# Two attention blocks on one core: scores with all maxima in one block, values in one run, and the steps around them moved

## The chip, the core and the metric

The kernel runs on one core of a Trainium2 chip. A core has five engines that run beside each other and wait for each other through semaphores: TensorE (PE in the profile) does matmuls into PSUM, VectorE (DVE) and ScalarE (ACT) work element by element and can read PSUM, GpSimd (POOL) works element by element in SBUF, and SyncE (SP) issues DMAs. Each engine takes its instructions strictly in the order of the program. The metric is the time of one execution on the device in microseconds.

## What is computed

`x` has 4 images of 64 channels by 32 x 32 positions. Two layers follow each other. Each one does this (cut from the reference of layer 0; layer 1 is the same but for the names and eps = 1e-6):

```python
h = group_norm(x, norm_w, norm_b)            # 32 groups, 2 channels each
q = einsum('bhwc,cd->bhwd', h, Wq) + bq      # k and v likewise
scores = einsum('bnc,bmc->bnm', qf, kf) * C ** (-0.5)     # 1024 x 1024 per image
attn = softmax(scores, axis=-1)
o = einsum('bnm,bmc->bnc', attn, vf)
o = einsum('bnc,cd->bnd', o, Wo) + bo
return x + o
```

## The kernel before

**Units.** An image in a layer is a unit; there are 8, numbered 0 to 7 (`LAST` = 7). A unit of the second layer needs the result of the same image in the first, four units earlier. The code runs in windows `w`: in window w the scores of unit w are computed, the maxima of unit w+1 and the preparation of unit w+2.

**A unit on TensorE.** The 1024 x 1024 scores are cut into 8 tiles of 128 keys by 1024 queries. `scores(u, t)` makes one tile by 8 matmuls (L846 to L863), six of them for the products of high and low parts of q and k and two that add the negative maximum of each query (`q_row`) to it. ScalarE then takes the exponential (`exp`, L442) from PSUM into `probs[t]`. `values(u, t)` (L878) multiplies the values with `probs[t]` and sums over the tiles in `ps_attn`. `project` and `project_v` make q, k and v of a unit from the normed image `h`.

**Maxima.** The maximum of each query has to be known before its scores tile is finished. `partial_max(u, m)` (L808, L809) computes one eighth of the scores in a single pass, and VectorE's `part` (L588) reduces it. All go through one PSUM buffer, `ps_max`, so that TensorE's next maximum waits for VectorE's reduction. After eight, `join` takes the maximum over the parts, TensorE turns the result (`turn_max`, L822), ScalarE stages it in `max_rows` (`stage_max`, L430), and SyncE's `place_rows` (L239) puts it into `q_row` by two DMAs.

**Denominators.** The sum of the eight `probs` of a unit is built by one addition on VectorE (`first_add`, L618, tiles 0 and 1) and six on GpSimd (`add`, L315, tiles 2 to 7; the code's number t is the tile's). An exponential of the next unit may write `probs[t]` only when the addition of the old one is done. `denominators` (L893) sums over the keys on TensorE after all six additions, `reciprocal` (L626) inverts on VectorE, and `spread_rden` sends the result to all channels by eight DMAs into `rden`: six issued by SyncE (L249) and two by ScalarE (L458), or all eight by SyncE for units 0 and 6. GpSimd's `finish` (L321, L324), the final step, multiplies by `rden` and adds the image. For units 5 to 7 VectorE does it (`finish_tail`, `finish_last`).

**Norm.** VectorE makes the statistics (`own_stats`, `share_stats`, `join_stats`), GpSimd takes the inverse square root (`root`, L296), VectorE makes gain and shift (`affine`), ScalarE applies them (`apply_norm`) and gives `h`.

**Order.** It is all written out by hand. On TensorE, in a window, scores, maxima and values alternate: two tiles of scores, a maximum, one to three tiles of values, and so on; tiles 6 and 7 of the values of unit w-1 come in window w. On GpSimd the root of unit w+2 comes first, then additions 2 to 5, `finish(w-1)`, additions 6 and 7. On SyncE comes `spread_rden(w-1)`, then the exchange DMAs of unit w+2 (`swap_hi`, `swap_lo`, which fill `cross`), then `place_rows(w+1)`.

Of the kernel before, what the change touches and what calls it, by code (L numbers as in the profile page):

```python
# [11 lines left out]
P = 128  # L12
# [18 lines left out]
def attention_pair(nc, x, layer_params, consts, out):  # L31
# [20 lines left out]
    with ExitStack() as ctx:  # L52
# [53 lines left out]
        ps_attn = psum("ps_attn", [P, HALF])  # L106
        ps_misc = psum("ps_misc", [P, HALF])
# [98 lines left out]

        def scores_buffer(unit, t):
            return ps_scores[t % 2] if unit < LAST else (ps_scores[0], ps_scores[1], ps_max)[t % 3]
# [4 lines left out]
        def _(sp):  # L213
# [53 lines left out]
            for w in range(UNITS):  # L267
                if w:
                    spread_rden(w - 1)
# [3 lines left out]
                if w + 1 < UNITS:  # L273
                    place_rows(w + 1)
# [6 lines left out]
        def _(pool):  # L281
# [53 lines left out]
            root(2)  # L335
            for w in range(UNITS):
                if 3 <= w + 2 < UNITS:
                    root(w + 2)
                for t in range(2, 2 + pool_adds(w)):
                    add(w, t)  # L340
                    if t == 5 and 0 < w < LAST - 1:
                        finish(w - 1)

        @block.scalar
        def _(act):
# [35 lines left out]
            def high_front(u):  # L381
                act.wait_ge(params_in[u // B], 16)
                act.wait_ge(proj_mm, u + 1)
                act.activation(front[u % RING][:, HI], ps_scores[0][:, HI], ACT.Identity,
                               bias=layer[u // B][:, BIAS_QK:BIAS_QK + 1]).then_inc(front_hi, 1)

            def high_back(u):
                act.wait_ge(back_set, u // B + 1)
                act.activation(back[u % RING][:, HI], ps_scores[0][:, LO], ACT.Identity,
# [87 lines left out]
            for w in range(UNITS):  # L477
                prep = w + 2 < UNITS
                exp(w, 0)
                exp(w, 1)  # L480
                if 0 < w < LAST:
                    copy_v(w + 1)
                if 0 < w < LAST:
                    copy_attn(w - 1)
                exp(w, 2)
                if w == LAST:
                    copy_attn(w - 1)
                exp(w, 3)
                if prep:
                    apply_norm(w + 2)  # L490
                exp(w, 4)
                exp(w, 5)
                if prep:
                    high_front(w + 2)
                    high_back(w + 2)
                if 1 < w < LAST:
                    spread_rden(w - 1)
                if 0 < w < LAST:
# [3 lines left out]
                exp(w, 6)  # L502
                exp(w, 7)
                if w == 0:
                    stage_max(1)
# [8 lines left out]
        def _(dve):  # L514
# [55 lines left out]
            def low_front(u):  # L570
                dve.wait_ge(front_hi, u + 1)
                dve.scalar_tensor_tensor(out=front[u % RING][:, LO], in0=ps_scores[0][:, HI],
# [4 lines left out]
            def low_back(u):  # L577
                dve.wait_ge(back_hi, u)
                dve.scalar_tensor_tensor(out=back[u % RING][:, LO], in0=ps_scores[0][:, LO],
# [4 lines left out]
            def part(u, m, ps=ps_max):  # L584
# [36 lines left out]
            def reciprocal(u):  # L621
                sums = ps_misc[:, 0:P] if u < LAST else ps_max[:, HALF:HALF + P]
# [74 lines left out]
            part(1, 0)  # L697
            own_stats(2)
            part(1, 1)
            share_stats(2)  # L700
            part(1, 2)
# [475 lines left out]
```

## Time and profile before

| | us |
|---|---|
| median of 3 runs | 186.3 (185.76 to 186.8) |
| the profiled execution | 186.09 |
| its span, from the first to the last instruction | 184.3 |
| TensorE busy | 177.0 (96%) |
| VectorE busy | 132.4 (72%) |
| GpSimd busy | 121.4 (66%) |
| ScalarE busy | 100.3 (54%) |

The span is what the trace shows; some 1.8 us of the execution lie outside it. The busy share of an engine alone does not say whether it bounds the kernel. The chain of waits does: it starts at the last instruction and goes back, at each step to whatever released it or to the instruction before it on its engine. The granted clock of TensorE was 0.997 of full speed on average.

### The profile page before, as it was taken

To read this page: it belongs to the slowest core of one execution; us is meant where nothing else is said; L and a number is where in the kernel's file an instruction comes from. 1 tells how busy PE (TensorE), PEld (TensorE's weight loads), DVE (VectorE), ACT (ScalarE), POOL (GpSimd) and SP (SyncE) were. 2 spreads that over 40 slices of the span, in tenths; PEclk is the share of its full clock that TensorE was granted. 3 is DMA by queue.
4 is the path that set the end of the run, shared out by engine and by line. 5 is a ranking of instruction groups with operands and counts; after the bars stand their busy time and mean duration, and the time that the engine had idled before them with its cause. 6 is when DMAs were issued, how large, how long until landed. Compare 5 with 4: busy or idle time off the path is not lost.

```text
span 184.3 us, 3436 instructions
## 1 busy us (share of the span) xinstructions
PE 177.0 (96%) x1295; PEld 96.2 (52%) x1295; DVE 132.4 (72%) x200; ACT 100.3 (54%) x137; POOL 121.4 (66%) x79
## 2 busy tenths in 40 slices
PE   7988899999999999999999999999999999999993
PEld 3445545545535655455535655555535555456671
DVE  2789987679867686859676785769675586484743
ACT  4289367616656376446666476426656554466500
POOL 3265016996799929997699949996799939705000
PEclk9999999999999999999999999999999999999998
DMA  5534100500025000420024001600025101010111
GB/s 152 190 78 107 43 5 0 114 4 2 0 50 124 3 0 18 114 44 0 4 70 102 0 0 31 146 4 0 1 66 111 57 0 46 16 57 16 44 57 57
DMA packets 8896, 8.90 MB, mean 48 GB/s; under 512 B 1656, under 2 KB 5936, under 8 KB 8880
## 3 DMA queue, kind: packets, MB, share of 16 engines
q1 hardware_dynamic: 7648, 7.90, 17.5%
q10 hardware_dynamic: 1232, 0.79, 1.5%
q8 instruction: 10, 0.16, 0.4%
q14 instruction: 6, 0.05, 0.1%
HBM read 1.58 MB, written 1.05 MB: 14 GB/s over the span
## 4 chain that ended last, share of the span: by engine, by line
PE 90%; DVE 8%; issue 1%; POOL 0%; ACT 0%; DVEq 0%; POOLq 0%
PE ps_attn L878 28%; PE ps_max L808 10%; PE ps_scores L846 8%; PE ps_scores L862 7%; PE ps_scores L850 7%; DVE part_max L588 7%; PE ps_scores L848 7%; PE ps_scores L787 4%; PE ps_scores L774 3%; PE ps_misc L795 3%; PE ps_misc L893 2%; PE ps_attn L885 2%; PE ps_misc L885 1%; PE ps_misc L822 1%; PE ps_scores L849 1%; PE ps_scores L863 1%
## 5 line engine op out<-in xcount | busy, mean ns | idle before, releaser
L315 POOL TENSOR_TENSOR prob_sum<-prob_sum,probs 128x1024 f32<-128x1024 f32 x41 | 97.6, 2379 | 29.0 <-ACT probs L442 16.8
L588 DVE TENSOR_REDUCE part_max<-ps_max 128x2 f32<-128x1024 f32 x60 | 73.4, 1223 | 31.3 <-PE ps_max L809 30.9
L442 ACT ACTIVATE probs<-ps_scores 128x1024 f32<-128x1024 f32 x62 | 61.0, 1026 | 46.1 <-PE ps_scores L863 45.4
L878 PE MATMUL ps_attn<-probs,vals 128*64 128x512 f32 x224 | 54.5, 605 | 0.0
L878 PEld LDWEIGHTS ps_attn<-probs,vals 128*64 128x64 f32 x224 | 13.5, 136 | 26.5 <-issue 17.9
L862 PE MATMUL ps_scores<-q_row,ones_r 64*128 64x512 f32 x62 | 24.5, 396 | 0.5 <-ACT q_row L424 0.5
L863 PE MATMUL ps_scores<-q_row,ones_r 64*128 64x512 f32 x62 | 24.6, 396 | 0.0
L808 PE MATMUL ps_max<-back,front 64*128 64x512 f32 x31 | 14.0, 450 | 1.4 <-DVE part_max L588 1.4
L808 PE MATMUL ps_max<-cross,front 64*128 64x512 f32 x29 | 14.7, 505 | 0.3 <-DVE part_max L588 0.3
L809 PE MATMUL ps_max<-cross,back 64*128 64x512 f32 x29 | 14.6, 505 | 0.0
L809 PE MATMUL ps_max<-front,back 64*128 64x512 f32 x31 | 14.0, 451 | 0.0
L296 POOL TENSOR_TENSOR rstd<-var_eps,minus_half 128x1 f32<-128x1 f32 x8 | 4.4, 554 | 13.4 <-DVE var_eps L543 13.4
L862 PEld LDWEIGHTS ps_scores<-q_row,ones_r 64*128 64x128 f32 x62 | 11.4, 184 | 3.2 <-issue 0.7
L847 PE MATMUL ps_scores<-back,cross 64*128 64x512 f32 x31 | 13.0, 418 | 0.0
L846 PE MATMUL ps_scores<-front,back 64*128 64x512 f32 x31 | 12.9, 416 | 0.0
L847 PE MATMUL ps_scores<-back,front 64*128 64x512 f32 x31 | 12.4, 400 | 0.0
L846 PE MATMUL ps_scores<-front,cross 64*128 64x512 f32 x31 | 12.4, 399 | 0.0
L851 PE MATMUL ps_scores<-back,cross 64*128 64x512 f32 x31 | 12.2, 392 | 0.0
L850 PE MATMUL ps_scores<-front,back 64*128 64x512 f32 x31 | 12.1, 391 | 0.0
L851 PE MATMUL ps_scores<-back,front 64*128 64x512 f32 x31 | 12.1, 390 | 0.0
L849 PE MATMUL ps_scores<-back,cross 64*128 64x512 f32 x31 | 12.1, 390 | 0.0
L850 PE MATMUL ps_scores<-front,cross 64*128 64x512 f32 x31 | 12.1, 390 | 0.0
(157 smaller groups left out, 365.8 us busy)
## 6 DMA issues: line engine op xcount, KB each, us to landing
cross<-front SPq DMA_DIRECT2D x16, 128.0 KB, 2.3
cross<-back SPq DMA_DIRECT2D x16, 128.0 KB, 2.3
rden<-block_rden SPq DMA_DIRECT2D x46, 32.0 KB, 1.9
xs<-x_dram SPq DMA_DIRECT2D x4, 256.0 KB, 4.6
out_dram<-xs SPq DMA_DIRECT2D x3, 256.0 KB, 2.0
rden<-block_rden ACTq DMA_DIRECT2D x10, 32.0 KB, 1.9
q_row<-max_rows SPq DMA_DIRECT2D x14, 2.0 KB
layer<-layers_dram SPq DMA_DIRECT2D x1, 194.5 KB, 2.6
```

What stands on the lines that cost most here:

```text
L315: pool.tensor_tensor(total[:, :], total[:, :], probs[t][:, :], ALU.add).then_inc(added, 1)
L442: act.activation(probs[t][:, :], scores_buffer(u, t)[:, :], ACT.Exp, scale=SCALE).then_inc(exp_done, 1)
L588: dve.tensor_reduce(part_max[u % 2][:, at:at + 2 * JS + 1:2 * JS], ps[:, :].rearrange("p (g n) -> p g n", g=2), AX.X, ALU.max, negate=True ...
L808: pe.matmul(ps[:, HI], f[top, tile], (x if crossed else g)[top, HI], start=True, stop=True)
L809: pe.matmul(ps[:, LO], g[low, tile], (x if crossed else f)[low, HI], start=True, stop=True).then_inc(max_mm, 1)
L846: pe.matmul(left, key_top[top, hi], front_u[top, HI], start=True, stop=False)
L847: pe.matmul(right, key_low[low, hi], back_u[low, HI], start=True, stop=False)
L850: pe.matmul(left, key_top[top, lo], front_u[top, HI], start=False, stop=False)
L851: pe.matmul(right, key_low[low, lo], back_u[low, HI], start=False, stop=False)
L862: pe.matmul(left, ones_r[top, :], row[top, :], start=False, stop=True)
L863: pe.matmul(right, ones_r[low, :], row[low, :], start=False, stop=True).then_inc(scores_mm, 1)
L878: mm = pe.matmul(ps_attn[half * C:(half + 1) * C, :], v, probs[t][:, cols], start=(t == 0), stop=(t == TILES - 1))
```

## The change

The change reorders the engines' programs and gives the maxima more PSUM buffers.

- **TensorE:** a window starts with one block in which the eight scores tiles of unit w alternate with the eight maxima of unit w+1. Then come the denominators of unit w-1 and one run of values 0 to 5 of unit w, the turn of the maxima, the projection, values 6, the projection of v, values 7.
- **PSUM:** `ps_attn` and `ps_misc` become the halves of one tensor, `ps_both`. Maxima 0, 2, 4 and 6 go to `ps_max`, 1, 3 and 5 to `ps_both`, 7 to `ps_scores[0]`. The projections from unit 2 on go to `ps_scores[1]`.
- **VectorE:** the first addition comes behind all eight reductions, and the statistics and the reciprocal behind it. In the tail the reciprocal of unit 6 comes behind two of the four late additions.
- **GpSimd:** the root of unit w+2 comes behind addition 2, the final step of unit w-1 behind addition 4 instead of 5.
- **ScalarE:** the eight exponentials in a row, everything else behind them.
- **SyncE:** `place_rows(w+1)` ahead of `spread_rden(w-1)`.

The diff, cut to its core:

```diff
-        ps_attn = psum("ps_attn", [P, HALF])
-        ps_misc = psum("ps_misc", [P, HALF])
+        ps_both = psum("ps_both", [P, N])
+        ps_attn = ps_both[:, 0:HALF]
+        ps_misc = ps_both[:, HALF:N]
...
+        def max_buffer(m):
+            return (ps_max, ps_both, ps_max, ps_both, ps_max, ps_both, ps_max, ps_scores[0])[m]
...
             for w in range(UNITS):
+                if w + 1 < UNITS:
+                    place_rows(w + 1)
                 if w:
                     spread_rden(w - 1)
                 if w + 2 < UNITS:
                     swap_hi(w + 2)
                     swap_lo(w + 2)
-                if w + 1 < UNITS:
-                    place_rows(w + 1)
...
             for w in range(UNITS):
-                if 3 <= w + 2 < UNITS:
-                    root(w + 2)
                 for t in range(2, 2 + pool_adds(w)):
                     add(w, t)
-                    if t == 5 and 0 < w < LAST - 1:
+                    if t == 2 and w + 2 < UNITS:
+                        root(w + 2)
+                    if t == 4 and 0 < w < LAST - 1:
                         finish(w - 1)
...
+                for t in range(TILES):
+                    exp(w, t)
                 if prep:
                     apply_norm(w + 2)
                 if 1 < w < LAST:
                     spread_rden(w - 1)
-                if 0 < w < LAST:
+                if w < LAST:
                     stage_max(w + 1)
                 if prep:
                     bias_x(w + 2)
+                    high_front(w + 2)
+                    high_back(w + 2)
+                    copy_v(w + 2)
+                if w < LAST:
+                    copy_attn(w)
...
+            for w in range(LAST):
                 prep = w + 2 < UNITS
+                part(w + 1, 0)
+                part(w + 1, 1)
+                for m in range(2, TILES):
+                    part(w + 1, m)
+                first_add(w)
+                join(w + 1, neg_max[:, :])
                 if prep:
                     own_stats(w + 2)
                     share_stats(w + 2)
                     join_stats(w + 2)
+                if w:
+                    reciprocal(w - 1)
                 if prep:
                     affine(w + 2)
                     low_front(w + 2)
                     low_back(w + 2)
+            pair_tail(LAST - 1)
             finish_tail(LAST - 2)
-            pair_tail(LAST - 1)
             add_tail(LAST - 1)
             first_add(LAST)
+            add_late(3)
+            add_late(4)
             reciprocal(LAST - 1)
-            for t in range(3, TILES - 1):
-                add_late(t)
+            add_late(5)
+            add_late(6)
             finish_tail(LAST - 1)
...
+            for w in range(LAST):
                 prep = w + 2 < UNITS
+                if w:
+                    next_max(w, 0)
+                    scores(w, 0)
+                for t in range(1, TILES - 3):
+                    next_max(w, t)
+                    scores(w, t)
+                scores(w, 5)
+                next_max(w, 5)
+                scores(w, 6)
+                next_max(w, 6)
+                scores(w, 7)
+                next_max(w, 7)
+                pe.wait_ge(max_done, TILES * (w + 1) + 6)
+                if w:
+                    denominators(w - 1)
                 values(w, 0)
                 values(w, 1)
                 values(w, 2)
                 values(w, 3)
                 values(w, 4)
                 values(w, 5)
+                if w:
+                    pe.wait_ge(rden_done, w)
+                turn_max(w + 1)
+                if prep:
+                    project(w + 2)
+                values(w, 6)
                 if prep:
                     pe.wait_ge(max_staged, w + 2)
                     project_v(w + 2)
+                values(w, 7)
```

How the instructions stand now, at three places. The first is SyncE's queue in a window of the steady part (w = 3). Before, in the order of the program:

```order
L249 DMA rden<-block_rden 64x1x128 x6
L222 DMA cross<-front 64x512
L224 DMA cross<-back 64x512
L229 DMA cross<-front 64x512
L231 DMA cross<-back 64x512
L239 DMA q_row<-max_rows 1x4x128 x2
```

Now:

```order
L246 DMA q_row<-max_rows 1x4x128 x2
L256 DMA rden<-block_rden 64x1x128 x6
L229 DMA cross<-front 64x512
L231 DMA cross<-back 64x512
L236 DMA cross<-front 64x512
L238 DMA cross<-back 64x512
```

The two row DMAs, which wait for the staged maxima, moved from the end of the window to its start, ahead of the spreading.

The second is GpSimd's queue in the same window; `rstd` is the root, `attn` and `xs` are the two instructions of the final step. Before:

```order
L296 TENSOR_TENSOR rstd<-var_eps,minus_half 128x1
L315 TENSOR_TENSOR prob_sum<-prob_sum,probs 128x1024 x4
L321 TENSOR_TENSOR attn<-attn,rden 128x512
L324 TENSOR_TENSOR xs<-attn,xs 128x512
L315 TENSOR_TENSOR prob_sum<-prob_sum,probs 128x1024 x2
```

Now, from the last four additions of the window ahead (its additions 5 to 7 and this window's addition 2):

```order
L322 TENSOR_TENSOR prob_sum<-prob_sum,probs 128x1024 x4
L303 TENSOR_TENSOR rstd<-var_eps,minus_half 128x1
L322 TENSOR_TENSOR prob_sum<-prob_sum,probs 128x1024 x2
L328 TENSOR_TENSOR attn<-attn,rden 128x512
L331 TENSOR_TENSOR xs<-attn,xs 128x512
```

The root moved behind addition 2, and three additions instead of two stand behind the final step.

The third is TensorE from the denominators to the turn of the maxima, in the same window. Before (scores in between left out):

```order
L893 MATMUL ps_misc<-prob_sum,parity 32x128 x8
L878 MATMUL ps_attn<-probs,vals 64x512 x2
L846 MATMUL ps_scores<-front,back 128x512
...
L787 MATMUL ps_scores<-h,layer 128x512
L789 MATMUL ps_scores<-h,back_w 128x512
L808 MATMUL ps_max<-cross,front 128x512
L809 MATMUL ps_max<-cross,back 128x512
L878 MATMUL ps_attn<-probs,vals 64x512 x6
L822 MATMUL ps_misc<-const_sb,neg_max 8x128
```

Now:

```order
L867 MATMUL ps_both<-prob_sum,parity 32x128 x8
L852 MATMUL ps_both<-probs,vals 64x512 x12
L791 MATMUL ps_both<-const_sb,neg_max 8x128
L756 MATMUL ps_scores<-h,layer 128x512
L758 MATMUL ps_scores<-h,back_w 128x512
L852 MATMUL ps_both<-probs,vals 64x512 x2
L764 MATMUL ps_both<-wvo,h 64x128 x8
L852 MATMUL ps_both<-probs,vals 64x512 x2
```

Scores and maxima are gone from between the denominators and the turn; six tiles of values stand there in a row.

## Rows read from the trace of the kernel before

**Rows 1.** The page, section 4: shares of the chain that ended last.
```profile
PE 90%; DVE 8%; issue 1%; POOL 0%; ACT 0%; DVEq 0%; POOLq 0%
```

**Rows 2.** Chain of waits, whole span: start, length, engine, tile, line, count.
```profile
47.36 0.57 PE ps_misc L893 x16
...
68.69 0.57 PE ps_misc L893 x16
...
150.42 0.57 PE ps_misc L893 x16
```

**Rows 3.** Chain of waits, one unit, from 88.9 to 109.8 us.
```profile
89.17 0.57 PE ps_misc L893 x16
89.74 1.01 PE ps_attn L878 x4
...
93.03 0.66 PE ps_scores L787
...
94.36 2.73 PE ps_attn L878 x12
...
101.68 0.87 PE ps_misc L795 x16
...
104.84 0.22 PE ps_max L808
...
106.94 0.43 PE ps_max L808
```

**Rows 4.** GpSimd in order of time: start, duration, instruction, count.
```profile
88.97 9.95 POOL L315 TENSOR_TENSOR prob_sum<-prob_sum,probs 128x1024 f32<-128x1024 f32 x4 [2.58 <-ACT probs L442]
98.88 1.29 POOL L321 TENSOR_TENSOR attn<-attn,rden 128x512 f32<-128x512 f32 x1
...
101.48 4.91 POOL L315 TENSOR_TENSOR prob_sum<-prob_sum,probs 128x1024 f32<-128x1024 f32 x2
106.34 0.56 POOL L296 TENSOR_TENSOR rstd<-var_eps,minus_half 128x1 f32<-128x1 f32 x1
```

**Rows 5.** SyncE in order of time, then TensorE's turn of the maxima.
```profile
152.58 3.95 SPq L249 DMA_DIRECT2D rden<-block_rden  x6
157.84 1.32 SPq L239 DMA_DIRECT2D q_row<-max_rows  x2
...
167.85 5.07 SPq L249 DMA_DIRECT2D rden<-block_rden  x8
...
157.18 0.27 PE L822 MATMUL ps_misc<-const_sb,neg_max 128*8 128x128 f32 x1
```

**Rows 6.** VectorE in the tail, in order of time; bracket: idle before, and releaser.
```profile
159.22 1.68 DVE L662 TENSOR_TENSOR attn<-attn,rden 128x512 f32<-128x512 f32 x1 [3.23 <-DMA rden<-block_rden]
...
175.83 0.69 DVE L662 TENSOR_TENSOR attn<-attn,rden 128x512 f32<-128x512 f32 x1 [0.72 <-DMA rden<-block_rden]
...
177.17 0.95 DVE L626 RECIPROCAL block_rden<-ps_max 128x128 f32<-128x128 f32 x1
```

**Rows 7.** The spreading DMAs (L249) from 152 to 160 us: time to landing.
```profile
DMA to landing us min/median/max: 1.8/2.0/3.3
```

**Rows 8.** The page, section 5, the reductions; then TensorE at the first scores.
```profile
L588 DVE TENSOR_REDUCE part_max<-ps_max 128x2 f32<-128x1024 f32 x60 | 73.4, 1223 | 31.3 <-PE ps_max L809 30.9
...
21.56 0.47 PE L862 MATMUL ps_scores<-q_row,ones_r 64*128 64x512 f32 x1 [0.46 <-ACT q_row L424]
```

**Rows 9.** VectorE, then ScalarE, in order of time, around 106 to 110 us.
```profile
106.44 1.22 DVE L618 TENSOR_TENSOR prob_sum<-probs 128x1024 f32<-128x1024 f32 x1
...
107.70 0.27 DVE L556 TENSOR_SCALAR shift<-mean_gain,rstd,layer 128x1 f32<-128x1 f32 x1
...
110.20 0.80 ACT L373 ACTIVATE h<-xs,shift,gain 128x512 f32<-128x512 f32 x1
```

**Rows 10.** Busy time by stretch: length, PE, PEld, DVE, ACT, POOL, clock, DMA.
```profile
181.00:182.00 1.00, 0.10 (x2) 0.00 (x0) 0.97 (x3) 0.00 (x0) 0.00 (x0) 1.00 0.00 0
...
183.00:184.30 1.30, 0.00 (x0) 0.00 (x0) 0.00 (x0) 0.00 (x0) 0.00 (x0) 0.57 0.30 101
```

More of the change, by code:

```diff
@@ L582, in low_back, with part @@
                                          op0=ALU.add, op1=ALU.subtract).then_inc(back_lo, 1)
-            def part(u, m, ps=ps_max):
+            def part(u, m, ps=None):
+                ps = ps if ps is not None else max_buffer(m)
                 crossed, j = divmod(m, JS)
@@ L621, in reciprocal @@
             def reciprocal(u):
-                sums = ps_misc[:, 0:P] if u < LAST else ps_max[:, HALF:HALF + P]
+                sums = ps_misc[:, 0:P] if u < LAST - 1 else ps_max[:, HALF:HALF + P]
                 dve.wait_ge(den_mm, u + 1)
@@ L717, in _ @@
-            share_stats(3)
-            join_stats(3)
-            part(2, 2)
-            first_add(1)
-            affine(3)
-            part(2, 3)
-            part(2, 4)
-            reciprocal(0)
-            part(2, 5)
-            part(2, 6)
-            part(2, 7)
-            join(2, neg_max[:, :])
-            low_front(3)
-            low_back(3)
-            part(3, 0)
-            part(3, 1)
-            for w in range(2, LAST):
-                prep = w + 2 < UNITS
+            for w in range(LAST):
+                prep = w + 2 < UNITS
+                part(w + 1, 0)
[4 more added lines that the diff above has]
+                join(w + 1, neg_max[:, :])
@@ L785, in project @@
                     pe.wait_ge(half_h, 1)
+                elif u >= HEAD:
+                    pe.wait_ge(exp_done, TILES * (u - 1))
                 first, second = slice(0, C), slice(C, P)
-                pe.matmul(ps_scores[0][:, HI], p[first, 0:P], h[first, :], start=True, stop=True)
+                pe.matmul(projected(u)[:, HI], p[first, 0:P], h[first, :], start=True, stop=True)
                 pe.wait_ge(back_set, u // B + 1)
-                pe.matmul(ps_scores[0][:, LO], back_w[u // B][second, :], h[second, :], start=True, stop=True).then_inc(proj_mm, 1)
+                pe.matmul(projected(u)[:, LO], back_w[u // B][second, :], h[second, :], start=True, stop=True).then_inc(proj_mm, 1)
             def project_v(u):
@@ L832, in scores_main @@
                     pe.wait_ge(*low_count(back_lo, head_back_lo, u))
+                    if u:
+                        pe.wait_ge(max_done, TILES * (u + 1))
+                if t == 1 and 0 < u < LAST:
+                    pe.wait_ge(front_lo, u)
+                    pe.wait_ge(back_lo, u)
                 g = TILES * u + t
@@ L1094, in _ @@
                     project_v(w + 2)
-            scores(LAST, 0)
-            scores(LAST, 1)
-            scores(LAST, 2)
-            values(LAST - 1, 6)
-            values(LAST - 1, 7)
-            pe.wait_ge(max_staged, UNITS)
-            denominators(LAST - 1)
-            scores(LAST, 3)
-            scores(LAST, 4)
-            scores(LAST, 5)
-            pe.wait_ge(rden_done, LAST)
+                values(w, 7)
+            for t in range(TILES):
+                scores(LAST, t)
+            pe.wait_ge(max_staged, UNITS)
             values(LAST, 0)
             values(LAST, 1)
-            scores(LAST, 6)
-            scores(LAST, 7)
+            denominators(LAST - 1)
             values(LAST, 2)
```

192 lines of the change are left out of this document (30 added, 162 removed).

## The prediction, made before the changed kernel ran

> **What bounds the kernel now.** First the page's shares of the chain of waits: the chain that ended last lies on TensorE for 90% [rows 1]. Then the chain in order of time. It gives the starts of the denominator sums, the once-per-unit step by which I measure everything: 47.36, 68.69, ..., 150.42 us [rows 2]. From 68.69 to 150.42 are four units, 20.4 us each. Inside one unit every piece of the chain is a TensorE piece that starts where the one before ends [rows 3]: no wait for another engine is in it. GpSimd is the next busiest. Its turn of one unit is 4 additions in 9.95 us, the two final-step multiplies and adds from 98.88 to 101.48, 2 additions in 4.91 us and a root of 0.56 us [rows 4]: 18.0 us of the 20.4. So GpSimd has 2.4 us of slack, and whatever it waits for beyond that becomes the time of the unit.
>
> **What the change makes wait.** I write T for the moment at which TensorE starts the denominators of unit w-1 in window w. They wait for all six GpSimd additions of unit w-1. Five edits form a ring from T(w) to T(w+1):
> 1. Denominators: 0.57 us to the first values tile [rows 3].
> 2. Six tiles of values in one run. The first takes 1.01 us, three take 2.73, so 0.91 each [rows 3]: 1.01 + 5 x 0.91 = 5.56 us.
> 3. The maxima are turned only now. From the turn at 157.18 to the first row DMA at 157.84: 0.66 us [rows 5].
> 4. On SyncE the row DMAs now stand ahead of the spreading of the reciprocals: 1.32 us [rows 5].
> 5. Six spreading DMAs follow. They began at 152.58 us [rows 5], and the multiply that waited for them started at 159.22 [rows 6]: 6.64 us. ScalarE's two go out before ScalarE turns to the staged maxima, and are earlier.
> 6. GpSimd, after addition 4, stands at the final step of unit w-1 until these land; additions 5, 6 and 7 of unit w are queued behind it. Final step 2.60 us, three additions at 9.95/4 = 2.48: 7.44 us [rows 4]. Hand-over 0.1 us, an estimate from the small gaps between rows.
> Sum: 0.57 + 5.56 + 0.66 + 1.32 + 6.64 + 2.60 + 7.44 + 0.1 = **24.9 us** for a unit, against 20.4. Before, additions 2 to 5 and the spreading ran side by side, and the final step found its data there: GpSimd shows no idle time before L321 [rows 4]. After, GpSimd reaches the final step about 9.4 us after T (first addition of VectorE 1.5, three additions 7.4, root 0.5), and the data come at 0.57 + 5.56 + 0.66 + 1.32 + 6.64 = 14.8 us. The wait is 5 to 6 us; the rest of it eats the old slack.
>
> **The landing is the softest term.** By its median a spreading DMA lands 2.0 us after its issue (1.8 to 3.3) [rows 7]. But both times an engine really waited it started later: the last issues stand one issue length (5.07/8 = 0.6) ahead of the ends of the queue's rows, at 155.9 and 172.3 us [rows 5], and VectorE began at 159.22 and 175.83 [rows 6], 3.3 and 3.5 us behind them. The 6.64 holds the long value, since my case is a waiting engine; with 2.0 the term is 5.3 and the ring 23.6. These two are the bounds. The Trainium skill (DMA: Bandwidth & Descriptors, section on the anatomy of one DMA) gives a fixed cost of about 2.0 us for setup and completion; by that the ring would be 23.6 and the total some 10 us lower than mine. The trace has the value where nobody waits and a longer one where somebody does.
>
> **The part before the ring.** Scores and maxima of the head stand in one block from 21.56 us on [rows 8]. Per tile TensorE needs 0.92 for the scores and 0.22 for a maximum [rows 3], VectorE 1.22 for a reduction [rows 8]. Seven more score tiles and maxima make 7 x 1.14 = 8.0, and I add 0.8 for the reductions' slower pace: values start at 30.4. The last reduction ends 1.5 us later; the first addition, now behind it, 1.22; GpSimd's addition 2.48; root 0.56 (now behind that addition); gain and shift 0.4; h 0.80 [rows 4, 9]. So h of unit 2 is ready 6.9 us after the values start, at 37.3, while TensorE has done its six tiles and the turn at 36.1 and stands. Projection 1.1 (from 93.03 to the values at 94.36, less a maximum of 0.22), values 0.91, value projection 0.87, values 0.91 [rows 3]: the next block begins at 41.1 and lasts another 9.8. T(1) = **50.9** against 47.36: +3.5 us.
> Window 1 differs from the ring: the stats and h come late (7.2 us after T to the staged maxima instead of 6.8), and SyncE issues all eight spreading DMAs, 167.85 to 175.83 = 7.98 us [rows 5, 6]. 7.2 + 1.32 + 7.98 + 2.60 + 7.44 + 0.1 = 26.6, T(2) = 77.5. Four rings of 24.9: T(6) = **177.1** against 150.42.
>
> **The tail.** From T(6): spreading issued after 8.1, landed 14.8; final step on VectorE 1.34 (175.83 to 177.17), tail addition and first addition 2.4: 18.5; GpSimd's one addition 2.48; two late additions, now ahead of the reciprocal, 2.4; reciprocal 0.95; eight spreading DMAs 7.98: 32.3; final step 1.34: 33.7. From the last reciprocal on the end is as before, 184.30 - 177.17 = 7.1 [rows 2, 6]: 40.8 us against 33.9. TensorE has nothing to do for about 5 us ahead of the last spreading. The granted clock averaged 0.57 in the last 1.3 us; TensorE had worked its last 0.1 us from 181 us on [rows 10]: I expect the low level, 1.2 GHz, for the last 1.8 us of work on the path, so +1.8.
>
> **Gains.** TensorE changes less often between kinds of matmul: a maximum right behind values takes 0.43 us of the chain, one within scores 0.22 [rows 3]. Some three changes fewer per unit would be 0.6 us. Maxima have two and three buffers now, so a reduction is no longer waited for. Both lie on TensorE, which waits for GpSimd anyway: nothing.
>
> **Sum.** The profiled execution took 186.09 us, its span 184.30, so 1.8 outside; it is 0.2 under the median of 186.3. Span after: 177.1 + 40.8 + 1.8 = 219.7; with 1.8 and 0.2: **221.7 us**. By differences: +3.5 head, +23.1 in the five windows (126.2 against 103.1), +6.9 tail, +1.8 clock.
>
> **Rivals.**
> A short landing (2.0 us instead of 3.3 to 3.5): less 1.5 + 4 x 1.3 in the windows and 1.3 + 1.5 in the tail: 212.2 us. For it: every landing that nobody waited for. Against it: both that somebody waited for.
> The clock falls within the units. TensorE is sparse while it waits for additions 5 to 7, with gaps of up to about 2.2 us, and the one fall of the trace began within about 2 us of its last matmul. Denominators and six tiles at 1.2 GHz are up to 6.1 us longer, and they are part of the ring: 5 x 6.1 = 31 at most, half of it likely: 237 us (226 to 252). Against it: the granted clock is full elsewhere, pauses of the head included.
> The ring does not close, because the reciprocals land before GpSimd is through addition 4. Then a unit lasts what GpSimd needs from block to block, 18.0 plus 2.6 for the late first addition = 20.6, about as before, and head, tail and clock remain: 186.3 + 3.5 + 6.9 + 1.8 = 198.5. Needs step 4 to cost nothing; the order of SyncE's queue speaks against it.
> Faster: the fewer changes of matmul kind decide. If all of steps 3 to 6 stay covered, and head and tail too, 6 units give 0.6 each, 182.7 us. It decides only where GpSimd's idle time stays under its 2.4 us of slack; I find 5 to 6.
>
> **Chances.** Forecast 0.53 (its own range 216 to 228), short landing 0.22, falling clock 0.15, no ring 0.06, faster 0.02, no change 0.02. The range takes in the first two and the lower part of the third, 207 to 234, which leaves a little under 2 in 10 out. Faster or slower means by over 0.5%, about what a measurement of this kernel can tell from no change: slower 0.96.
>
> **What would show it.** In the profile after: GpSimd idle ahead of the attn multiply in windows 1 to 5, released by the DMA of rden, 5 to 6 us each; denominator sums 24 to 26 us apart; the chain of waits going through GpSimd and SyncE instead of lying on TensorE; ScalarE's exponentials 5, 6 and 7 waiting for additions; VectorE's tail waiting for rden twice. Right steps with a ring of 23.6 is the short landing. Pairs of values matmuls well over 0.91 us a tile, with a granted clock under 1, is the third case. If GpSimd goes from addition 4 straight into the final step, the forecast is wrong at its root.

## The result, and the profile after

The changed kernel took **217.5 us** (median of 4 runs, 214.89 to 219.88) against 186.5 for the kernel before: 1.155 times as long, 95% interval 1.148 to 1.163. (The ratio, and the differences between versions below, use only executions within 1.5% of the fastest of their kernel; here these are 214.89 and 215.84, median 215.4.) The profiled execution took 215.84 us and its span is 214.0. The parts that follow are counted in spans: 214.0 against 184.3, **+29.7 us**.

The page first: its chain of waits by engine, the group of the waiting multiply, and the granted clock in 40 slices.

```profile
PEclk9999999999999999999999999995799969999688
...
POOL 36%; issue 19%; PE 19%; DVE 13%; SPq 4%; DMA 3%; ACT 3%; POOLq 1%; DVEq 0%; ACTq 0%
...
L328 POOL TENSOR_TENSOR attn<-attn,rden 128x512 f32<-128x512 f32 x5 | 6.4, 1286 | 23.4 <-DMA rden<-block_rden 23.4
```

TensorE's share of the chain fell from 90% [rows 1] to 19%, and GpSimd's rose from nothing to 36%. GpSimd's busy time hardly changed (121.6 us against 121.4), but 23.4 us of idle time now stand ahead of the five multiplies by `rden`. The clock row has three dips: at 145 to 155 us, at 171 to 176 and in the last 16.

Then T, the start of the denominators in windows 1 to 6, from TensorE's order of time (start, duration, instruction, count; in brackets the idle time before and what ended it):

```profile
50.74 0.64 PE L867 MATMUL ps_both<-prob_sum,parity 128*32 128x128 f32 x16
...
75.59 0.65 PE L867 MATMUL ps_both<-prob_sum,parity 128*32 128x128 f32 x16 [0.94 <-POOL prob_sum L322]
...
99.00 0.64 PE L867 MATMUL ps_both<-prob_sum,parity 128*32 128x128 f32 x16 [0.95 <-POOL prob_sum L322]
...
122.31 0.64 PE L867 MATMUL ps_both<-prob_sum,parity 128*32 128x128 f32 x16 [0.96 <-POOL prob_sum L322]
...
146.70 1.08 PE L867 MATMUL ps_both<-prob_sum,parity 128*32 128x128 f32 x16 [0.37 <-POOL prob_sum L322]
...
172.95 1.08 PE L867 MATMUL ps_both<-prob_sum,parity 128*32 128x128 f32 x16 [0.94 <-POOL prob_sum L322]
```

The windows last 24.9, 23.4, 23.3, 24.4 and 26.2 us. In three parts, against [rows 2]:

| part | before | after | difference | predicted difference |
|---|---|---|---|---|
| up to T(1) | 47.4 | 50.7 | +3.4 | +3.5 |
| five windows | 103.1 | 122.2 | +19.1 | +23.1 |
| from T(6) to the end | 33.9 | 41.1 | +7.2 | +8.7, of it 1.8 for the clock |

The chain of waits over window 3 (start, length, what) is no longer the row of TensorE pieces of [rows 3]:

```profile
99.23 1.23 DVE prob_sum L613
...
100.60 2.36 POOL prob_sum L322
...
103.43 2.36 POOL prob_sum L322
...
105.93 2.37 POOL prob_sum L322
108.30 3.82 issue
...
112.16 1.29 POOL attn L328
...
114.79 2.34 POOL prob_sum L322
```

It runs from VectorE's late first addition through GpSimd's additions 2 to 4, then 3.82 us of nothing, then the final step (L328, L331) and the three additions queued behind it, of which the first is shown. What GpSimd waits for in the 3.82 us is seen in TensorE's and SyncE's order of time. The same steps before are in [rows 5]:

```profile
99.57 5.37 PE L852 MATMUL ps_both<-probs,vals 128*64 128x512 f32 x24
104.87 0.27 PE L791 MATMUL ps_both<-const_sb,neg_max 128*8 128x128 f32 x1
...
105.58 1.35 SPq L246 DMA_DIRECT2D q_row<-max_rows  x2
107.03 3.80 SPq L256 DMA_DIRECT2D rden<-block_rden  x6
...
130.33 3.81 SPq L256 DMA_DIRECT2D rden<-block_rden  x6
134.18 1.41 SPq L229 DMA_DIRECT2D cross<-front  x1
```

The values end, the maxima are turned at 104.87, the row DMAs go out at 105.58, and only then the spreading (L256) at 107.03. The last of its six issues starts one issue before 110.83, at 110.2, and GpSimd starts at 112.16, 1.9 us behind it. So the ring is there, edge for edge: 0.57 + 5.3 + 0.71 + 1.45 + 5.13 + 2.59 + 7.42 + 0.14 = 23.3 us. These are in turn the denominators, the values, turn to row DMAs, rows to spreading, spreading to final step, the final step, three additions, the hand-over to T(4) = 122.31.

The windows 1 to 5 and the tail by stretch (length, PE, PEld, DVE, ACT, POOL, granted clock, DMA share and GB/s), and below them three stretches around T(5) = 146.70 (windows 1 and 2 read as window 3, but for their length):

```profile
98.90:122.20 23.30, 20.17 (x149) 11.11 (x149) 15.16 (x24) 12.25 (x15) 17.21 (x9) 1.00 0.15 35
122.20:146.60 24.40, 20.77 (x149) 11.19 (x149) 14.61 (x24) 12.35 (x15) 17.18 (x9) 0.97 0.15 34
146.60:172.90 26.30, 23.03 (x149) 11.83 (x149) 15.79 (x24) 12.35 (x15) 17.18 (x9) 0.89 0.16 41
172.90:214.00 41.10, 30.66 (x241) 17.42 (x241) 18.30 (x21) 9.96 (x12) 12.59 (x5) 0.87 0.11 33
...
144.00:146.00 2.00, 0.47 (x2) 0.29 (x2) 0.00 (x0) 1.02 (x1) 1.86 (x2) 0.80 0.02 4
146.00:148.00 2.00, 1.63 (x20) 0.95 (x20) 1.63 (x2) 1.02 (x1) 0.55 (x1) 0.50 0.00 0
...
152.00:154.00 2.00, 2.00 (x12) 0.70 (x10) 0.16 (x1) 0.81 (x1) 2.00 (x1) 1.00 0.07 16
```

In windows 1 to 3 the granted clock is full, 2.4 GHz. From 146 to 152 us, in window 5, it is 0.50, the 1.2 GHz level. TensorE had worked 0.47 of the 2 us from 144 to 146, and the clock fell in that stretch. It fell again around T(6): 0.62 from 172 to 174 and 0.52 from 174 to 176.

The tail, by its chain of waits (start, length, what):

```profile
172.95 1.08 PE ps_both L867 x16
174.03 6.25 PE ps_both L852 x24
...
185.52 1.84 DMA rden<-block_rden
187.39 0.70 DVE attn L657
...
202.05 1.89 DMA rden<-block_rden
...
206.31 1.71 PE ps_max L905 x16
208.01 2.82 PE ps_both L859 x16
```

### The profile page after: what moved, and what is told of

The parts are those of the page before. It is cut to its first block, busy times and chain, and to the rows that moved or that the text cites. A ratio compares the mean times of both kernels' runs of the same rounds, so it can differ in the third digit from the quotient of the medians.

```text
span 214.0 us, 3456 instructions
## 1 busy us (share of the span) xinstructions
PE 181.0 (85%) x1295; PEld 99.9 (47%) x1295; DVE 132.8 (62%) x200; ACT 103.3 (48%) x137; POOL 121.6 (57%) x79
## 4 chain that ended last, share of the span: by engine, by line
POOL 36%; issue 19%; PE 19%; DVE 13%; SPq 4%; DMA 3%; ACT 3%; POOLq 1%; DVEq 0%; ACTq 0%
POOL prob_sum L322 29%; DVE prob_sum L613 4%; PE ps_both L852 4%; DVE part_max L583 4%; SPq L256 4%; POOL attn L328 3%; POOL xs L331 3%; ACT probs L448 2%; PE ps_scores L820 2%; DMA rden<-block_rden 2%; PE ps_scores L777 2%; PE ps_scores L822 2%; PE ps_scores L836 2%; PE ps_scores L824 1%; PE ps_both L859 1%
## 5 line engine op out<-in xcount | busy, mean ns | idle before, releaser
L852 PE MATMUL ps_both<-probs,vals 128*64 128x512 f32 x224 | 55.2, 629 | 0.0
L583 DVE TENSOR_REDUCE part_max<-ps_max 128x2 f32<-128x1024 f32 x32 | 39.2, 1225 | 13.1 <-PE ps_max L778 13.1
L583 DVE TENSOR_REDUCE part_max<-ps_both 128x2 f32<-128x1024 f32 x21 | 25.8, 1226 | 7.2 <-PE ps_both L778 7.2
L852 PEld LDWEIGHTS ps_both<-probs,vals 128*64 128x64 f32 x224 | 15.3, 144 | 29.4 <-issue 28.2
L836 PE MATMUL ps_scores<-q_row,ones_r 64*128 64x512 f32 x62 | 24.5, 395 | 0.5 <-ACT q_row L430 0.5
L583 DVE TENSOR_REDUCE part_max<-ps_scores 128x2 f32<-128x1024 f32 x11 | 13.4, 1223 | 10.1 <-PE ps_scores L778 10.1
L328 POOL TENSOR_TENSOR attn<-attn,rden 128x512 f32<-128x512 f32 x5 | 6.4, 1286 | 23.4 <-DMA rden<-block_rden 23.4
L379 ACT ACTIVATE h<-xs,shift,gain 128x512 f32<-128x512 f32 x7 | 5.7, 812 | 26.8 <-DVE shift L550 26.8
L566 DVE SCALAR_TENSOR_TENSOR front<-ps_scores,layer,front 128x512 fp32r<-128x512 f32 x6 | 4.5, 751 | 20.3 <-ACT front L390 20.3
L821 PE MATMUL ps_scores<-back,cross 64*128 64x512 f32 x31 | 13.2, 427 | 0.0
L821 PE MATMUL ps_scores<-back,front 64*128 64x512 f32 x31 | 12.3, 398 | 0.0
L825 PE MATMUL ps_scores<-back,cross 64*128 64x512 f32 x31 | 12.1, 392 | 0.0
L825 PE MATMUL ps_scores<-back,front 64*128 64x512 f32 x31 | 12.1, 391 | 0.0
L823 PE MATMUL ps_scores<-back,front 64*128 64x512 f32 x31 | 12.1, 390 | 0.0
```

The lines of the kernel that those rows point to most:

```text
L328: pool.tensor_tensor(a[:, :], a[:, :], rden[:, :], ALU.mult).then_inc(normed, 1)
L583: dve.tensor_reduce(part_max[u % 2][:, at:at + 2 * JS + 1:2 * JS], ps[:, :].rearrange("p (g n) -> p g n", g=2), AX.X, ALU.max, negate=True ...
L821: pe.matmul(right, key_low[low, hi], back_u[low, HI], start=True, stop=False)
L823: pe.matmul(right, key_low[low, hi], back_u[low, LO], start=False, stop=False)
L825: pe.matmul(right, key_low[low, lo], back_u[low, HI], start=False, stop=False)
L836: pe.matmul(left, ones_r[top, :], row[top, :], start=False, stop=True)
```

## Experiments

Each run is compared with runs of the kernel before on the same chip (medians 185.7 to 186.3). Edits are shown against the changed kernel unless said otherwise; "window" means from T to T.

**1. Undoing only the order on SyncE.** If the ring is the cause, one moved line opens it.

```diff
             for w in range(UNITS):
-                if w + 1 < UNITS:
-                    place_rows(w + 1)
                 if w:
                     spread_rden(w - 1)
+                if w + 1 < UNITS:
+                    place_rows(w + 1)
```

> One part undone: on SyncE the spreading of the reciprocals goes ahead of the row DMAs again (the exchange DMAs stay last). Theory A, the ring through SyncE's queue: spreading starts at the reciprocal, 4.5 us behind T, and lands about 9.8, when GpSimd is just through addition 4. Windows 2 to 5 go from 23.4 (24.4 and 26.3 with the fallen clock) to about 20.8 us, window 1 from 24.8 to 22; the total to 196 to 200 us. Theory B, GpSimd is starved by the late first addition (the longest waits of its page, 35.5 us): nothing of that changes, so under 1 us. Theory C, the fallen clock is the loss: at most the 4 us that it costs in windows 4 and 5.

Measured: 195.52 us, ratio 1.052 (1.046 to 1.058), half a microsecond under the expected 196 to 200. Windows 22.0, 20.6, 20.6, 20.6 and 21.6. SyncE in window 3, then GpSimd in window 2, in order of time:

```profile
98.60 3.80 SPq L256 DMA_DIRECT2D rden<-block_rden  x6
102.44 1.31 SPq L246 DMA_DIRECT2D q_row<-max_rows  x2
...
78.19 4.87 POOL L322 TENSOR_TENSOR prob_sum<-prob_sum,probs 128x1024 f32<-128x1024 f32 x2
83.15 1.29 POOL L328 TENSOR_TENSOR attn<-attn,rden 128x512 f32<-128x512 f32 x1
```

The spreading is out before the rows are, and GpSimd goes from addition 4 into the final step with no bracket, so it does not wait. This edit alone takes away 20 of the 29 us (215.4 to 195.5, against 186.5). The block form with this order has a steady window of 20.6 us, as long as the old one of 20.4 within 0.2.

**2. and 3. The final step further back on GpSimd.** The same ring, opened at its other end: fewer additions behind the final step. The condition `t == 4` becomes `t == 5`, then `t == 7`.

```diff
-                    if t == 4 and 0 < w < LAST - 1:
+                    if t == 5 and 0 < w < LAST - 1:
                         finish(w - 1)
```

> One part undone: GpSimd's final step stands behind addition 5 again, so that two additions instead of three follow the wait. Theory A: GpSimd reaches it 11.9 us behind T, still ahead of the landing at 13.4, so each of five windows loses exactly one addition, 2.48 us: -12.4, with the clock's share -13 to -16, 200 to 203 us. Theory B: no change, the additions are as many and start as late.

> The final step of unit w-1 behind addition 7, so that no addition stands behind the wait and the ring is cut while SyncE's order stays as changed. Theory A: a unit lasts what TensorE or GpSimd need, 20.4 to 20.8 us; total 195 to 200 us. Theory B: no change but for the order of the waits, over 212 us.

Measured: 202.23 (1.083, 1.077 to 1.090) behind 5, as expected. Behind 7 it was 201.91 (1.082, 1.077 to 1.087): no further gain, a **miss**. The idle time ahead of L328 was 23.4 us in all in the changed kernel and is 8.4 behind 5. Behind 7 GpSimd does not wait for `rden` at all, and the chain takes another way around, through the same queue (chain of waits, 94 to 117 us):

```profile
95.36 1.23 DVE prob_sum L613
...
103.15 0.62 SPq L256
...
107.64 3.61 DMA cross<-back
...
111.39 0.47 PE ps_max L777
```

The exchange DMAs of unit w+2 stand behind rows and spreading. The maxima that come next on TensorE (L777) need them, and now they come last. (This landing took 3.61 us; the median for `cross` is 2.3 on the page of the changed kernel.) The chain enters SyncE's queue through VectorE's late first addition, GpSimd's addition 2 and root, ScalarE's `h` and the staged maxima behind it, so this second ring, unlike the first, contains the first addition. The order of SyncE's queue closes two rings: one through GpSimd's additions, one through `cross`. Moving the final step opens only the first. The page of the changed kernel already had this wait, 5.0 us in 5 times; I had overlooked it.

**4. The first addition back behind reduction 3.** Is the late first addition on the path?

```diff
                     part(w + 1, m)
-                first_add(w)
+                    if m == 3:
+                        first_add(w)
```

> One part undone: VectorE's first addition stands behind reduction 3 of the block again instead of behind all eight. Theory A: GpSimd starts earlier and waits that much longer at the final step; windows unchanged within 0.3 us, only the head gains about 1.5 us: 213 to 217 us. Theory B: each window loses the 1.7 us that GpSimd waits for the addition, 5 x 1.7 and the head: 204 to 207 us.

Measured: 224.19 us (1.198, 1.190 to 1.207), slower than the changed kernel by 8.7 (215.4 to 224.1). A **miss**, and of the sign at that. Windows 25.3, 26.5, 27.0, 25.6 and 26.7. Two things came in. First, GpSimd (chain of waits), then VectorE (order of time):

```profile
94.36 3.35 POOL prob_sum L322
...
93.63 1.81 DVE L613 TENSOR_TENSOR prob_sum<-probs 128x1024 f32<-128x1024 f32 x1
```

The first addition on VectorE reads two operands from SBUF, and it now runs beside GpSimd's addition 5. Of the two, VectorE takes 1.81 instead of 1.22, GpSimd 3.35 instead of 2.37: 1.0 us more in the ring. Second, the granted clock over 51 to 182 us was 0.91. Windows 2, 3 and 5 began at the low level: in window 2, denominators and values took 1.08 + 7.25 us instead of 0.64 + 5.37, 2.3 more. Five times 1.0 and three times 2.3 are 11.9 us; the five windows are 13.0 us longer than with a full clock in the changed kernel (131.1 against 24.9 + 4 x 23.3).

**5. Two more DMA issues between rows and spreading.** It measures the slope: whatever stands there should lengthen each window by its own length.

```diff
                     place_rows(w + 1)
+                if 0 < w < LAST:
+                    for n in range(2):
+                        sp.dma_start(spare[n * JS:(n + 1) * JS, :],
+                                     consts[n * JS:(n + 1) * JS, 0:P]).then_inc(spared, 16)
                 if w:
                     spread_rden(w - 1)
```

> One cost doubled: in windows 1 to 6 SyncE issues two more DMAs of 2 KB (from DRAM to a spare tile nobody reads) between the row DMAs and the spreading. Theory A: SyncE's issue time lies in the ring with slope one, 2 x 0.65 = 1.3 us in each of six windows: +7.8 us, 222 to 226 us. Theories B and C: SyncE's queue has room, no change.

Measured: 221.81 us (217.90 to 225.42, too far apart for a ratio), just under the expected 222 to 226. Execution for execution it is less than that: 217.90, the profiled one, is 2.5 over 215.4, so the size is a **miss**. Windows of the profiled one: 25.7, 24.2, 25.6, 24.9 and 24.4 us. SyncE in its window 2:

```profile
84.50 0.79 SPq L281 DMA_DIRECT2D spare<-consts_dram  x2
85.40 3.84 SPq L258 DMA_DIRECT2D rden<-block_rden  x6
```

The two issues with their gap took 0.9 us, not the 1.3 I had set. Windows 1 and 2 grew by 0.8 each. The others are held against a window of 23.3 us with a full clock. Window 3 grew by 2.3: the clock fell at its start, and the row DMAs came 8.0 us after T instead of 6.6, which is 1.4 of it. Window 4 grew by 1.6, of which 0.8 lies in its six spreading issues (4.57 us instead of 3.81), and window 5 by 1.1. What is left each time is 0.8 to 1.1, so the slope is about 1.

**6. Work for TensorE in its waits.** Five short matmuls without use, in windows 2 to 6: three ahead of the last maximum, two ahead of the denominators.

```diff
                 scores(w, 7)
-                next_max(w, 7)
                 pe.wait_ge(max_done, TILES * (w + 1) + 6)
+                if w > 1:
+                    keep_warm(3)
+                next_max(w, 7)
+                if w > 1:
+                    keep_warm(2)
```

> Filler matmuls (their results are overwritten, nothing reads them): three ahead of the last maximum and two ahead of the denominators in windows 2 to 6, where TensorE waits; all else as changed. Theory A with the clock as a second cause: windows 4 and 5 go from 24.4 and 26.3 to 23.4 us, about -4, and the clock is full until the tail: 210 to 213 us. If the clock costs nothing, no change; if the fillers come in the way, up to +2.

Measured: 210.38 us (1.130, 1.127 to 1.133), as expected. The clock over the five windows, one answer by stretch:

```profile
50.80:171.10 120.30, 114.14 (x801) 61.36 (x800) 76.78 (x116) 61.38 (x76) 86.07 (x45) 1.00 0.16 36
```

Windows 24.9, 23.5, 24.4, 23.6 and 23.9, where the changed kernel had 24.9, 23.4, 23.3, 24.4 and 26.2. The clock was worth 5.0 us (215.4 to 210.4). In the profiled executions the span is 5.4 shorter: 2.0 in the five windows (window 5 alone gave back 2.4) and 3.6 behind T(6), where the clock is now full. Without a fallen clock windows 2 to 5 are still 23.5 to 24.4: the ring does not need the clock.

**7. The reciprocal of unit 6 ahead of the late additions,** as it stood before.

```diff
             first_add(LAST)
+            reciprocal(LAST - 1)
             add_late(3)
             add_late(4)
-            reciprocal(LAST - 1)
```

> One part undone: in the tail the reciprocal of unit 6 stands ahead of all late additions again. The spreading starts 3.4 us earlier (at 193.7 instead of 197.1 us): 211 to 213.5 us if the tail's path goes through the reciprocal as predicted; no change if the late additions set it.

Measured: 213.62 us (1.146, 1.143 to 1.149). That is 0.1 over the expected 211 to 213.5, and 2.2 under the changed kernel (215.4 to 213.2). Run 6 is the fair comparison for the tail, since both have a full clock at T(6): the first of the eight spreading issues comes 19.4 us after T(6) instead of 22.8, because the two late additions of 2.5 us are back behind the reciprocal, and the tail is 35.6 us instead of 37.5.

**8. Three edits together:** the final step behind 7 (3), the first addition early (4), the reciprocal first (7).

> Three together: final step behind addition 7, first addition behind reduction 3, reciprocal of unit 6 ahead of the late additions. If theory A holds and nothing new binds: 190 to 196 us, still slower than before, since the tail's late denominators of unit 6 and SyncE's order stay. Below 186 would show that the block form is worth something by itself.

Measured: 193.53 us (1.039, 1.037 to 1.042), inside the bounds. The same early first addition that cost 8.7 us in run 4 helps here: with the final step behind 7 alone (run 3) the five windows take 111.6 us, of them 24.0 in one whose clock fell for a time (0.93), and here 105.7. The second ring contains this addition, and in window 3 the row DMAs come 6.5 us after T instead of 7.6. GpSimd from 96 us on:

```profile
96.83 12.43 POOL L322 TENSOR_TENSOR prob_sum<-prob_sum,probs 128x1024 f32<-128x1024 f32 x5
109.22 2.28 POOL L328 TENSOR_TENSOR attn<-attn,rden 128x512 f32<-128x512 f32 x1
```

VectorE's first addition of this window took 2.66 us from 107.68 on, beside the last of the five additions and the multiply L328, which took 2.28 instead of 1.29. The collision is still there, but the final step waits for nothing and none of the unit's additions stands behind it, and the windows stay at 20.3 to 21.9 us.

**9. Run 4 with the waits filled as in run 6.** It parts the two causes of run 4.

```diff
-                first_add(w)
+                    if m == 3:
+                        first_add(w)
...
+                if w > 1:
+                    keep_warm(3)
+                next_max(w, 7)
+                if w > 1:
+                    keep_warm(2)
```

> The early first addition with the filler matmuls in TensorE's waits (nothing reads their results), to divide the early addition's loss of about 7 us. Clock share: denominators and six values tiles at 1.2 GHz cost 2.4 us in each of windows 2 to 5 without fillers. Shared access: where VectorE's first addition runs beside GpSimd's addition 5, the latter took 3.35 us instead of 2.37, so +1.0 us in each ring, which fillers can't mend. If both hold: full clock up to the tail, windows 24.3 to 24.6 us, 213 to 217 us. If the clock is all of it: windows 23.4 and 210 us, as with the fillers alone. If neither: 222 us or more.

Measured: 215.69 us (1.160, 1.153 to 1.166), with the clock at 0.99 from 51 to 177.6 us. Windows 25.4, 24.3, 27.3, 24.5 and 24.8. The fillers give back 8.4 of run 4's 224.1 us. Against run 6 (210.4) the early first addition costs 5.3. In windows 1, 2, 4 and 5 it is 0.5 to 0.9 each, which fits the collision of 1.0 us. Window 3 is 2.9 longer; it also has a SyncE issue of 1.46 us, and the clock fell in it once more (0.50 from 124 to 126 us). The first ring does not pass through the first addition, and placing it earlier gains nothing while that ring is closed.

**10. Runs 1 and 7 together.**

> SyncE's spreading ahead of the row DMAs and, in the tail, the reciprocal of unit 6 ahead of the late additions; all else as changed. The two repairs lie in different stretches and should add up: 195.5 less 3 to 4 us, 191.5 to 193 us, still over the kernel before by the head (3.4 us) and the rest of the tail.

Measured: 194.81 us (1.047, 1.042 to 1.052), 0.7 under run 1 where 3 to 4 were expected, a **miss**. The reciprocal came 2.2 us earlier (175.40 against 177.57), but then TensorE stands longer ahead of its last matmuls (4.36 us against 3.81) and works longer at the low level. Run 12 below shows it.

**11. The kernel before with only the row DMAs moved ahead of the spreading.** The converse of run 1, the edit shown against the kernel before.

```diff
             for w in range(UNITS):
+                if w + 1 < UNITS:
+                    place_rows(w + 1)
                 if w:
                     spread_rden(w - 1)
...
-                if w + 1 < UNITS:
-                    place_rows(w + 1)
```

> One part of the change alone, made in the kernel before: SyncE's row DMAs ahead of the spreading. Theory A: the ring closes there too, with two additions behind the final step: in the kernel before the staged maxima come some 8.5 us behind the denominators (118.1 against 109.6), rows 1.3, spreading 5.2, final step 2.6, two additions 4.9: 22.5 to 23 us a window against 20.5, 196 to 201 us. If the order of SyncE's queue matters only in the block form: 186 to 188 us.

Measured: 223.43 us (1.200, 1.195 to 1.205), more than the whole change. The direction is right, the size a **miss** by over 20 us. Windows 28.9, 27.1, 27.2, 27.9 and 24.5. Its chain of waits from 102 to 131 us:

```profile
112.82 5.10 issue
...
117.96 1.28 POOL attn L321
...
120.61 0.69 DVE stats L522
...
123.28 0.01 PE ps_max L809
```

Addition 5, a wait of 5.1 us, the final step: the same ring. Then it goes on to VectorE's statistics of unit w+2 (L522), which read the image that the final step has just written. In the old order these statistics stand between the reductions of the same window, so all maxima, and TensorE with them, wait as well. The page of waits lists it with 25.7 us in 4 times. On top comes the clock: 8 matmuls of values took 3.61 us, where 8 at the full clock in the same window took 1.94. In the block form the statistics stand behind all reductions, and this second part of the damage is absent.

**12. Run 10 with nine short matmuls ahead of the last denominators.** Shown against run 10.

```diff
                 pe.wait_ge(rden_done, LAST)
+                pe.wait_ge(exp_done, TILES * UNITS)
+                keep_warm(9, ps_scores[1])
                 pe.wait_ge(late_added, TILES - 4)
```

> As the run with both repairs (194.8 us), with nine filler matmuls (3.9 us, results never read) where TensorE waits for the last late additions, 177.2 to 181.6 us. In that run the reciprocal of unit 6 came 2.2 us earlier and the span ended only 0.5 us earlier; TensorE's last values tiles took 3.58 us at a granted clock of 0.50. If the clock took the gain: full clock there, tiles in 1.9 us, 192.7 to 193.5 us. If the reciprocal's path had little to give in itself: 194.5 to 195 us.

Measured: 193.39 us (1.040, 1.037 to 1.043), as expected. The last values of run 10, then of run 12:

```profile
183.43 3.58 PE L859 MATMUL ps_both<-probs,vals 128*64 128x256 f32 x16
```

```profile
182.12 1.95 PE L859 MATMUL ps_both<-probs,vals 128*64 128x256 f32 x16
```

Sixteen matmuls of 3.58 us at a granted clock of 0.50 took 1.95 at 1.00. That is where 1.4 us of the gain missing in run 10 had gone (194.8 to 193.4). No version beat the kernel before. Run 12 has ring and clock mended and its span is still 7.1 us longer: the head +3.4 (T(1) = 50.76), the five windows +1.9 (T(6) = 155.76), the tail +1.7.

## Why the prediction was right, and where it was off

**The ring was the right mechanism.** Predicted 221.7, measured 217.5, inside the forecast's own range of 216 to 228. GpSimd waits ahead of the multiply in windows 1 to 5, as said (3.86 to 6.24 us each, where I had 5 to 6), the denominators are 23 to 26 us apart, and the chain runs through GpSimd and SyncE. Run 1 opens the ring and gets 20 us, run 2 opens it at the other end and gets 13, run 5 lengthens it and the windows follow, run 11 builds it into the other kernel.

**The mis-sized term was the landing, step 5.** I took 6.64 us from the first spreading issue to the final step, because both waits of the trace of before had a landing of 3.3 to 3.5 us [rows 5, 6]. It was 5.13 in window 3, with a landing of 1.9. Window 1, with eight issues, took from 59.03 to 65.45 = 6.42 instead of 7.98. The tail's two waits for `rden` had 1.84 and 1.89 in the chain above. So what I called the short landing, the bound of 5.3 and a ring of 23.6, was the better value: "Both that somebody waited for" was two cases, and of the seven waits of the changed kernel only one was like them (window 4: last issue at 133.54, final step at 136.54, 3.0 us). Why some are long I cannot say. I should have kept to the median of 2.0 us. The short landing took 0.4 to 1.6 us off each window, 6.1 in all, and 2.7 off the tail.

The Trainium skill (DMA: Bandwidth & Descriptors, section "Anatomy of one DMA") gives a fixed cost of about 2.0 us; it measured that on DMAs that GpSimd issues. The six other waits here, on DMAs of SyncE, agree with it at 1.9 us each.

**The rival with the low clock came true in part, and filled the gap.** By the short landing alone I had 212.2 us. The profiled execution came out 3.6 us above it (215.84), and run 6 with its filled waits gives 210.4. The dip at T(5) made window 5 longer by 2.5 us (the row DMAs came 9.1 us after T instead of 6.6), another 0.4 lies in its DMAs; the dip at T(6) delayed the tail by 1.3. I had priced a fall at up to 6.1 us and in five windows at once, 226 to 252 in all; it is a matter of single windows, at 2.5. Two errors of opposite sign, the long landing put in and the falls of the clock in the windows left out, made the sum look better than its terms. That it came within 2% is in part luck.

**The other steps.** Denominators, values and turn: 6.6 us to the row DMAs against 6.79. Rows to spreading 1.45 against 1.32. Final step and additions 10.01 against 10.04. Head: values from 30.18 (30.4 predicted), next block from 40.79 (41.1), T(1) = 50.74 (50.9). In the tail the first spreading issue comes 9.4 us after T(6) instead of 8.1, because the denominators and the first of the six tiles ran at the low level (1.08 + 6.25 us in the chain). The short landing took that back, GpSimd's addition ends at 20.6 (21.0), the reciprocal starts at 23.2 (23.4), the eight issues and their landing are 6.83 (7.98). From the last reciprocal to the end it is 8.7 us against 7.1 + 1.8: of these, the last spreading matmuls (L905) 1.71 and the last values 2.8 at the low level, as forecast.

**What I left out.** The step through `cross` (runs 2 and 3) did no harm in the changed kernel because the first ring is longer, but it bounds what moving the final step can gain, and it makes the place of the first addition matter (run 8). And in window 4 a single SyncE issue after the spreading took 1.41 us instead of 0.59 (SyncE's rows above), `rden` landed later and the window lasted 1.1 us more.

**The rivals that fell.** That the ring does not close: run 1 shows what that would have been, 195.5 against my 198.5. Its windows are 2.2 us longer than before in sum (I had nothing for them), its tail only 3.3, since the spreading of unit 5 is out early there too. That fewer changes of matmul kind decide: the steady window without the ring is 20.6 us, no shorter than 20.4.

## What to carry to other kernels

A DMA queue is a program like that of an engine. Before something is put ahead of something else in it, write down what the moved DMA waits for, and follow whether that in turn hangs on what is now behind it: two row DMAs of 1.3 us cost 20 us because they carried a wait with them. A ring is found by walking from one step of the unit back to the same step of the next, and its length is the sum of its edges, whatever the busy shares are. When a wait has been opened, look for the second one right behind it (run 3), and for what the change of timing makes collide (run 4).

## What the runs showed of the hardware

**VectorE and GpSimd slow each other when both read two operands from SBUF.** In run 4 the addition on VectorE took 1.81 instead of 1.22 and GpSimd's 3.35 instead of 2.37. In the tail of the changed kernel the first late addition (L635) stands beside GpSimd's; in run 1 the final step of unit 5 (L657, L660) does:

```profile
175.26 2.71 DVE L635 TENSOR_TENSOR late_sum<-probs 128x1024 f32<-128x1024 f32 x1
```

```profile
164.82 2.58 DVE L657 TENSOR_TENSOR attn<-attn,rden 128x512 f32<-128x512 f32 x1 [2.69 <-DMA rden<-block_rden]
167.44 2.78 DVE L660 TENSOR_TENSOR xs<-attn,xs 128x512 f32<-128x512 f32 x1
```

2.71 us instead of 1.22, 2.58 and 2.78 instead of 0.69. The 1.68 of [rows 6] is of the same kind: GpSimd's addition there ran until 160.35 us, 1.13 after the multiply's start, and 0.55 of the 1.68 is left. Reductions from PSUM and reciprocals beside the same additions keep their 1.22 and 0.95. The Trainium skill (SBUF — State Buffer, section Terms) describes a port pair that the two engines share as a lock, held for a whole instruction. The losses shown here agree: each (at most 2.09 us on VectorE, 1.0 on GpSimd) is shorter than one instruction of the other engine (2.37 and 1.22).

**TensorE's clock drops within the steady part.** At T(5) of the changed kernel it fell to the 1.2 GHz level in a stretch in which TensorE worked 0.47 of 2 us, with 1.60 us idle at one time, and it stayed there until 152 us, although TensorE was busy all of the time from 148 on; the window was 2.5 us longer for it. With five short matmuls in the waits of a window it stayed at 2.4 GHz in all windows of run 6, with nine in the tail wait in run 12. In run 9, with the same five, it still fell once.

**Now and then a SyncE issue takes 1.3 to 1.9 us instead of 0.6.** It was one or two exchange DMAs behind the spreading in the profiled executions of the changed kernel and of runs 2 to 9 and 11; it can also be a spreading DMA (1.3 us in the kernel before and in run 1, 1.9 in run 3). Where it was an exchange DMA right behind the spreading (window 4 of the changed kernel, window 3 of runs 6 and 9), the final step started 1 to 1.6 us later. The cause is open. So is that of the long landings of before.
